# Experts' rows by a scatter in DRAM and VectorE transposes in place of gathers and TensorE transposes, one core of Trainium2

## The chip, the core and the metric

One core of a Trainium2 chip runs the kernel. The metric is the device time in microseconds of one execution. Before the change the median of three runs is 691.87 us (689.24 to 692.97).

## What is computed

Four sequences of 512 tokens with 512 channels go through one layer: a linear attention whose state is trained step by step (a recurrence over 32 mini batches of 16 tokens), a layer norm, then a mixture of eight experts of which each token takes two, beside a shared expert, and a second layer norm.

```python
k, v = heads(x @ Wk.T), heads(x @ Wv.T)           # 16 heads of 32, k rotated
def step(W, (kc, vc)):                             # 32 steps of 16 tokens
    z = kc @ W
    return W - kc.T @ ((z - vc) * inv_n), z
x = layernorm(x + (layernorm(zs) * gamma + beta) @ Wo.T)
probs = softmax(x @ w_gate); w, ids = top_k(probs, 2); w /= sum(w)
expert_e(x) = (silu(x @ gate_e) * (x @ up_e)) @ down_e          # 512 -> 2*256 -> 512
routed = sum over the two experts of w * expert(x)
shared = (silu(x @ g) * (x @ u)) @ down_sh                      # 512 -> 2*1024 -> 512
out = layernorm(x + routed + shared)
```

## The kernel before

All products of the large matrices are made in a fast 32-bit form from a high and a low part: each operand is split by ScalarE (a copy that rounds, "high") and VectorE or GpSimd (the difference, "low"), and TensorE multiplies high by high, high by low and low by high. 24 products of 128x128 by 128x512 are thus one half of a gate block, twelve one bank.

The 2048 tokens are 16 tiles of 128 rows, `x1[:, i, :]`. One function, `stages()`, writes the order of all steps by hand, and each engine's function walks through the same list and issues its own part of every step; so a step's place in the list is its place in the queue of every engine that has a part in it, SP's and GpSimd's too. Signals (`mark`, `on`) tie them together.

1. Recurrence, steps n = 0 to 71. At step n a tile i has its parts at n - 4i = 3 (rows, z), 4 (turn), 5 (statistics, which go through DRAM and back on SP), 7 (output product), 8 (`mix`), 9 (`x1`), 10 (`x1 turn`, TensorE turns the tile for the router), 11 (`logits`). `LAST = 4 * NT - 4 + 11` is the last step. From n = 47 on a budget per step (`SCAN`, `DRAIN`) lets the generator `shared()` lay products of the shared expert between; in the last steps it is 2.3 a step and 2.0 more at one. A half gate or a down product costs 1.3 of it.
2. Routing, `route(e, rt)`, pieces 0 to 18, laid between the products of the shared expert, nearly all on VectorE. Pieces 0 to 7 pick two experts for each token and count them (TensorE sums the counts in piece 7), 8 to 11 give each expert tiles, 12 gives each token its two slots (`SI`, line 867) and weights (`WW`). Pieces 13 to 16 build one-hot matrices from the slots, TensorE multiplies them in two groups of 16 (line 1213, pieces 17 and 18), and the product is the inverse list, `idxu`: which token sits in which slot.
3. Experts. There are 22 tiles of slots, eight wide (four strips of 128 rows) and 14 narrow (one strip); the first seven narrow ones stand between the wide ones in `ORDER`, 15 jobs with 39 strips, and a narrow tile that is not used is skipped by a branch (its products are left out, its strip is still fetched, turned and split). The other seven are rare and have a branch of their own, not entered here. With these inputs five of the narrow jobs have tokens (jobs 1, 3, 5, 7, 9); 11 and 13 have none. For each strip s, step `gather` makes GpSimd fetch 128 rows of `x1d` through `idxu` into one of four places of `xg` (line 1805); step `rows turn` has TensorE turn them into a PSUM bank by four transposes (line 1255), ScalarE copy the high part from there into `RH` or `XH1` (line 1712) and VectorE take the low part (line 1491). A wide job's strips go to the buffer of parity p, and their first copy waits for the gates of the wide job before, which read the same buffer (`row_left`).
   In a job TensorE does the gates (`rows gate`, line 1268: four banks in 2 x 24 products; `strip gate`, line 1281: 12), and then the down products of the job before (`rows down`, line 1305: six for a strip). ScalarE copies each down product out of bank 6 or 7 (line 1726) and SP writes it to `yd` (line 1042). VectorE multiplies gate and up parts (lines 1450, 1496) and takes low parts (1452, 1500); ScalarE and VectorE split the gate weights (1654, 1440), ScalarE and GpSimd the down weights (1659, 1792). During a wide job the one strip of the next narrow job is turned, during a narrow job the four of the next wide job.
4. The last shared products for tiles 8 to 15; GpSimd gathers each token's two rows of `yd` through `SI` (line 1830), VectorE adds them (1508), and the last layer norm ends it.

SP's issues stand in its queue in the order of the list: it waits for a step's signal and only then looks at the next.

## Time and profile before

| | before |
|---|---|
| median of three runs | 691.87 us |
| the profiled execution | 693.32 us |
| its span (first to last instruction) | 691.5 us |
| TensorE busy | 666.4 us |
| VectorE busy | 428.3 us |
| ScalarE busy | 298.9 us |
| GpSimd busy | 295.3 us |
| mean granted clock of TensorE | 0.989 |
| moved by DMA | 92.47 MB |

The profile is of one execution; it took 1.8 us more than its span and stands 1.45 us above the median of the runs. Busy times are of instructions; a matmul's end is modelled, so it is the distance between the starts of two groups that tells how long a group takes. The chain of waits is followed back from the last instruction.

### The profile page before, as it was taken

What the parts mean: (1) busy time and instruction counts of PE and PEld (TensorE: products, weight loads), DVE (VectorE), ACT (ScalarE), POOL (GpSimd) and SP (SyncE); (2) the same over time, 40 slices, a digit from 0 to 9 for tenths busy, and PEclk for the clock granted to TensorE, in tenths of its full rate; (3) what the DMA queues carried; (4) which work ended last, traced back from release to release, by engine and by line L of the source; (5) the groups of instructions that cost most, each with busy time, mean ns of one, the idle gap of its engine ahead of it and who ended that gap; (6) DMA issues with size and microseconds to landing.
All of it is one profiled execution on the core that took longest, in us unless ns stands there. A gap on an engine that the chain in (4) does not pass through costs nothing.

```text
span 691.5 us, 16510 instructions
## 1 busy us (share of the span) xinstructions
PE 666.4 (96%) x6880; PEld 534.6 (77%) x6880; DVE 428.3 (62%) x750; ACT 298.9 (43%) x520; POOL 295.3 (43%) x308
## 2 busy tenths in 40 slices
PE   9889999998999999999999999999999999999994
PEld 7656777776777777787887888888887888888883
DVE  5787766776845345488866544554456267676655
ACT  5534434542654432441123456655677442142232
POOL 0745666766736531011005335343552244726232
PEclk9989999999999999999999999999999999999998
DMA  8210152232351532100063578667657765414212
GB/s 283 83 65 20 50 174 80 85 109 63 112 171 50 171 98 91 45 1 0 1 244 114 177 265 299 199 245 256 207 161 259 261 185 175 123 61 127 72 76 91
DMA packets 65710, 92.47 MB, mean 134 GB/s; under 512 B 16672, under 2 KB 31776, under 8 KB 65632
## 3 DMA queue, kind: packets, MB, share of 16 engines
q1 hardware_dynamic: 59952, 72.76, 31.2%
q0 software_dynamic: 5680, 18.62, 9.5%
q8 instruction: 56, 0.92, 0.5%
q14 instruction: 22, 0.18, 0.1%
HBM read 67.56 MB, written 23.79 MB: 132 GB/s over the span
## 4 chain that ended last, share of the span: by engine, by line
PE 54%; DVE 18%; POOL 9%; issue 7%; ACT 5%; DMA 4%; SPq 0%; DVEq 0%; POOLq 0%; ACTq 0%
PE bank L1305 7%; PE zbank L1268 6%; PE wbank L1268 6%; PE zbank L1181 5%; PE bank L1073 4%; PE bank L1128 4%; PE wbank L1181 4%; PE bank L1194 3%; DVE x L1460 3%; POOL xg L1830 2%; DMA xg<-yd,SI 2%; PE zbank L1281 2%; DVE x L1508 2%; PE bank L1181 2%; PE zbank L1091 2%
## 5 line engine op out<-in xcount | busy, mean ns | idle before, releaser
L1792 POOL TENSOR_TENSOR xl<-RAW,xh 128x1024 fp32r<-128x1024 f32 x23 | 55.5, 2412 | 122.7 <-ACT xh L1659 122.6
L1675 ACT ACTIVATE ah<-sg 128x512 fp32r<-128x512 f32 x48 | 30.3, 632 | 158.4 <-DVE sg L1450 158.4
L1805 POOL DMA_INDIRECT xg<-x1d,idxu x39 | 42.0, 1078 | 69.8 <-DVE idxu L892 41.3
L1440 DVE TENSOR_TENSOR GL<-RAW,GH 128x1024 fp32r<-128x1024 f32 x42 | 50.3, 1223 | 11.0 <-ACT GH L1654 9.6
L1452 DVE TENSOR_TENSOR al<-sg,ah 128x512 fp32r<-128x512 f32 x48 | 34.1, 711 | 33.5 <-ACT ah L1675 33.5
L1194 PE MATMUL bank<-xh,ah 128*128 128x512 f32 x128 | 51.2, 400 | 1.7 <-DVE x L1460 1.0
L1830 POOL DMA_INDIRECT xg<-yd,SI x32 | 35.4, 1106 | 38.6 <-DVE x L1508 24.1
L1073 PE MATMUL bank<-xh,GH 128*128 128x512 f32 x112 | 49.0, 438 | 2.4 <-DVE shuf L1346 2.4
L1194 PE MATMUL bank<-xh,al 128*128 128x512 f32 x128 | 49.9, 390 | 0.0
L1194 PE MATMUL bank<-xl,ah 128*128 128x512 f32 x128 | 49.9, 390 | 0.0
L1450 DVE TENSOR_TENSOR sg<-sg,zbank 128x512 f32<-128x512 f32 x22 | 15.1, 685 | 53.1 <-PE zbank L1268 36.4
L1073 PE MATMUL bank<-xl,GH 128*128 128x512 f32 x112 | 45.6, 407 | 0.1
L1654 ACT ACTIVATE GH<-RAW 128x1024 fp32r<-128x1024 f32 x44 | 45.2, 1056 | 0.0
L1073 PE MATMUL bank<-xh,GL 128*128 128x512 f32 x112 | 45.1, 403 | 0.0
L1460 DVE TENSOR_TENSOR x<-bank,x 128x512 f32<-128x512 f32 x64 | 40.9, 680 | 5.9 <-PE bank L1194 5.8
L1181 PE MATMUL zbank<-XH,GH 128*128 128x512 f32 x112 | 44.1, 394 | 0.2 <-DVE XL L1445 0.2
L1181 PE MATMUL wbank<-XH,GH 128*128 128x512 f32 x112 | 43.8, 391 | 0.0
L1181 PE MATMUL zbank<-XH,GL 128*128 128x512 f32 x112 | 43.6, 389 | 0.0
L1181 PE MATMUL wbank<-XH,GL 128*128 128x512 f32 x112 | 43.6, 389 | 0.0
L1181 PE MATMUL wbank<-XL,GH 128*128 128x512 f32 x112 | 43.6, 389 | 0.0
L1181 PE MATMUL zbank<-XL,GH 128*128 128x512 f32 x112 | 43.6, 389 | 0.0
L1588 ACT ACTIVATE W<-wbank 128x512 f32<-128x512 f32 x31 | 18.5, 597 | 41.7 <-PE wbank L1107 41.7
(302 smaller groups left out, 1773.3 us busy)
## 6 DMA issues: line engine op xcount, KB each, us to landing
RAW<-in_wgu SPq DMA_DIRECT2D x13, 1024.0 KB, 6.5
yd<-RAW SPq DMA_DIRECT2D x39, 256.0 KB, 4.7
RAW<-in_wsgu SPq DMA_DIRECT2D x14, 512.0 KB, 5.1
RAW<-in_wd SPq DMA_DIRECT2D x13, 512.0 KB, 5.8
x<-in_xtok SPq DMA_DIRECT2D x16, 256.0 KB, 3.4
x1d<-x SPq DMA_DIRECT2D x16, 256.0 KB, 2.3
RAW<-in_wsd SPq DMA_DIRECT2D x8, 512.0 KB, 4.8
out_x<-x SPq DMA_DIRECT2D x16, 256.0 KB, 2.0
```

What stands on the lines that cost most here:

```text
L1073: t = e.matmul(bank[b][:], (WL if wl else WH)[:, j, k, hg * 128:hg * 128 + 128], (xl if xlo else xh)[:, k, :], start=(k == 0 and not wl an ...
L1181: t = e.matmul(bank[b][:], (GL if wl else GH)[:, w % 2, k, c:c + 128], (XL if xlo else XH)[q % 2][:, k, :], start=(k == 0 and not wl and n ...
L1194: t = e.matmul(bank[b][:], (al if al_ else ah)[:, ap, k, j * 128:j * 128 + 128], (DL if wl else DH)[:, w % 2, k, :], start=(k == 0 and not ...
L1268: t = e.matmul(bank[b][:], (GL if wl else GH)[:, w % 2, k, c:c + 128], (rowl if xlo else rowh)[p][:, k, :], start=(k == 0 and not wl and n ...
L1305: t = e.matmul(bank[b][:], (al if al_ else ah)[:, p, k, h * 128:h * 128 + 128], (DL if wl else DH)[:, w % 2, k, :], start=(k == 0 and not ...
L1440: e.tensor_tensor(GL[:, w % 2, k:k + 2, :], gate_raw(w, k), GH[:, w % 2, k:k + 2, :].bitcast(F32), ALU.subtract).then_inc(*mark("low", "g" ...
L1452: e.tensor_tensor(al[:, ap, fc, :], sg[:, g, :], ah[:, ap, fc, :].bitcast(F32), ALU.subtract).then_inc(*mark("low", "a", w, q, fc))
L1460: e.tensor_tensor(x1[:, i, :], bank[b][:], x1[:, i, :], ALU.add).then_inc(*mark("acc", w, q, j))
L1654: e.activation(GH[:, w % 2, k:k + 2, :], gate_raw(w, k), ACT.Copy).then_inc(*mark("high", "g", w, k))
L1792: e.tensor_tensor(DL[:, w % 2, :, :], draw[:, raw_of(w), :, :], DH[:, w % 2, :, :].bitcast(F32), ALU.subtract).then_inc(*mark("low p", "d" ...
L1805: e.indirect_dma_start(place(s), None, x1d, bass.IndirectOffsetOnAxis(ap=idxu[:, LINES[s]:LINES[s] + 1], axis=0)).then_inc(*mark(f"dma xg{ ...
L1830: e.indirect_dma_start(xg[:, p, j, :], None, yd, bass.IndirectOffsetOnAxis(ap=SI[:, j, i:i + 1], axis=0)).then_inc(*mark(f"dma ya{p}", i, j))
```

## The change

Instead of the inverse list, the rows themselves are put in the experts' order: as soon as the slots are known (piece 12), GpSimd writes the rows of all 16 tiles through `SI` into an array `xsd` in DRAM, once for each of the two experts: 32 indirect DMAs, tiles 8 to 15 from `x1`, tiles 0 to 7 (whose `x1` has shared products added by then) from a copy reloaded into the two row buffers, first slots before second ones. Slots that no token takes hold rows that SP writes during the recurrence: each finished tile is also written to up to three of the 46 lines of `xsd`. A strip is then a plain read of 128 rows: SP loads it by four DMAs, the quarter g of the channels to the 32 partitions from 32g, so that transposes of 32x32 blocks on VectorE are enough to bring the channels onto the partitions, in an order to which the rows of the gate weights are permuted on the host. VectorE turns the strip into one of two buffers `xt`, ScalarE and VectorE split it from there. The 39 groups of four transposes, pieces 13 to 18 of the routing with their 32 products, and the gathers of `x1d` are gone.

The first four strips are loaded after the scatter and after the loads of weights of jobs 0 and 1; a strip s + 4 is loaded when strip s is turned. In the list a strip's split comes behind the turn of the next one.

The last tile of the recurrence has `mix` and `x1` in the same step as its output product and its turn and logits in the two steps behind, so there are two steps fewer (`LAST` 69 instead of 71), with their budget of fill work.

```diff
-LAST = 4 * NT - 4 + 11
+LAST = 4 * NT - 4 + 9
-        tiles = {d: (n - d) // 4 for d in range(3, 12) if (n - d) % 4 == 0 and 0 <= (n - d) // 4 < NT}
+        tiles = {d: (n - d) // 4 for d in range(3, 12) if (n - d) % 4 == 0 and 0 <= (n - d) // 4 < NT - (d > 7)}
+        if n >= 4 * NT + 4:
+            tiles.update({10: NT - 1} if n == LAST - 1 else {11: NT - 1})
...
             do("wo", tiles[7], left[7])
+            if tiles[7] == NT - 1:
+                do("mix", NT - 1)
+                left[7] = ("mix", NT - 1)
+                do("x1", NT - 1)
...
-        for q_, at in ((0, 49), (1, 69)):
+        for q_, at in ((0, 49), (1, 66)):
...
-        budget += 0 if n < 47 else SCAN[n % 4] if n < 64 else DRAIN + 2.0 * (n == LAST - 2)
+        budget += 0 if n < 47 else SCAN[n % 4] if n < 64 else DRAIN + 1.4 * (n == LAST - 2)
...
-    route, pause = list(range(19)), 0
-    pauses = {6: 1, 16: 6}
+    route, pause = list(range(13)), 0
+    pauses = {6: 1}
...
-            if r == 18:
-                left[4] = ("routed", "index")
-                for s in range(4):
-                    do("gather", s, None)
+            if r == 12:
+                do("scatter")
...
+    for s in range(4):
+        do("rows in", s)
+    def turn_rows(j):
         p = j % 2
         for h, line in enumerate(strips(ORDER[j])):
-            b, s = banks[h], AT_LINE[j] + h
-            do("rows turn", s, p, h, b, left[b], row_left[p])
-            left[b] = ("low", "r", s)
-            place_left[s % 4] = ("turned", "r", s)
+            s = AT_LINE[j] + h
+            do("rows turn", s)
+            if h:
+                do("rows split", s - 1, p, h - 1, row_left[p])
             if s + 4 < len(LINES):
-                do("gather", s + 4, place_left[s % 4])
+                do("rows in", s + 4)
             yield
+        do("rows split", s, p, h, row_left[p])
...
SP:
                 elif step == "x1":
                     i, = a
                     e.wait_ge(*on("x1", i))
+                    for line in range(3 * i, min(3 * i + 3, COLS)):
+                        e.dma_start(xsd[128 * line:128 * line + 128, :], x1[:, i, :]).then_inc(*mark(f"dma x1d{i // 4}", "x", line))
...
                     e.dma_start(ups[:], upd).then_inc(*mark("dma table"))
+                    for h in range(2):
+                        e.wait_ge(*on(f"dma x1d{h}", 4 * h + 3))
+                        e.dma_start(early[h], x1d[512 * h:512 * h + 512, :].rearrange("(t p) n -> p t n", p=128)).then_inc(*mark(f"dma early{h}", h))
...
+                elif step == "rows in":
+                    s, = a
+                    if s == 0:
+                        for j in range(2):
+                            e.wait_ge(*on(f"dma xs{j}", 7))
+                    if s >= 4:
+                        e.wait_ge(*on("rows", s - 4))
+                    for g in range(4):
+                        e.dma_start(place(s)[32 * g:32 * g + 32, :].rearrange("p (m c) -> p m c", m=4),
+                                    xsd[128 * LINES[s]:128 * LINES[s] + 128, 128 * g:128 * g + 128].rearrange("(m i) c -> i m c", m=4)).then_inc(*mark(f"dma xq{s % 4}", s, g))
...
TensorE:
-                elif step == "rows turn":
-                    s, p, h, b, free, after = a
-                    e.wait_ge(*on(f"dma xg{s % 4}", s))
-                    e.wait_ge(*on(*free))
-                    for g in range(4):
-                        t = e.transpose(bank[b][:, g * 128:g * 128 + 128], place(s)[:, g * 128:g * 128 + 128], ident[:])
-                    t.then_inc(*mark("turned", "r", s))
...
VectorE:
                 elif step == "rows turn":
+                    s, = a
+                    e.wait_ge(*on(f"dma xq{s % 4}", s, 3))
+                    if s > 1:
+                        e.wait_ge(*on("low", "r", s - 2))
+                    e.transpose(xt[:, s % 2, :].rearrange("p (c m i) -> p m c i", c=4, m=4), place(s).rearrange("p (m c i) -> p m c i", m=4, c=4)).then_inc(*mark("rows", s))
+                elif step == "rows split":
+                    s, p, h, after = a
                     e.wait_ge(*on("high", "r", s))
-                    e.tensor_tensor(rowl[p][:, :, h * 128:h * 128 + 128], bank[b][:].rearrange("p (a b) -> p a b", a=4),
+                    e.tensor_tensor(rowl[p][:, :, h * 128:h * 128 + 128], xt[:, s % 2, :].rearrange("p (a b) -> p a b", a=4),
                                     rowh[p][:, :, h * 128:h * 128 + 128].bitcast(F32), ALU.subtract).then_inc(*mark("low", "r", s))
...
ScalarE:
+                elif step == "rows split":
+                    s, p, h, after = a
+                    e.wait_ge(*on("rows", s))
                     if h == 0 and after:
                         e.wait_ge(*on(*after))
-                    e.activation(rowh[p][:, :, h * 128:h * 128 + 128], bank[b][:].rearrange("p (a b) -> p a b", a=4), ACT.Copy).then_inc(*mark("high", "r", s))
+                    e.activation(rowh[p][:, :, h * 128:h * 128 + 128], xt[:, s % 2, :].rearrange("p (a b) -> p a b", a=4), ACT.Copy).then_inc(*mark("high", "r", s))
...
GpSimd:
-                elif step == "gather":
...
+                elif step == "scatter":
+                    for q in range(4):
+                        e.wait_ge(*on(f"dma x1d{q}", 4 * q + 3))
+                    for j in range(2):
+                        e.wait_ge(*on("routed", "slots", j))
+                        for i in (*range(8, NT), *range(8)):
+                            if j == 0 and i in (0, 4):
+                                e.wait_ge(*on(f"dma early{i // 4}", i // 4))
+                            rows = early[i // 4][:, i % 4, :] if i < 8 else x1[:, i, :]
+                            e.indirect_dma_start(xsd, bass.IndirectOffsetOnAxis(ap=SI[:, j, i:i + 1], axis=0), rows, None).then_inc(*mark(f"dma xs{j}", i))
```

## Rows read from the trace of the kernel before

**Rows 1.** The page: busy us, share of the span, instructions, of TensorE.
```profile
PE 666.4 (96%) x6880; PEld 534.6 (77%) x6880; DVE 428.3 (62%) x750; ACT 298.9 (43%) x520; POOL 295.3 (43%) x308
```

**Rows 2.** TensorE's waits, 260 to 400 us: total us, times, longest.
```profile
PE zbank L1268 <- DVE RL L1491: 0.6, 1, 0.6
```

**Rows 3.** The chain of waits: start us, us, what.
```profile
357.21 1.70 PE bank L1213 x16
...
379.60 5.69 PE zbank L1268 x24
...
391.23 0.44 PE bank L1255 x4
...
401.47 5.48 PE zbank L1268 x24
...
458.92 1.36 PE bank L1305 x6
...
460.72 2.77 PE zbank L1281 x12
...
470.53 5.48 PE zbank L1268 x24
...
504.96 1.36 PE bank L1305 x6
...
513.97 5.48 PE zbank L1268 x24
```

**Rows 4.** VectorE in order of time: start us, us, instruction, idle before.
```profile
292.95 0.28 DVE L734 TENSOR_REDUCE red<-logits 128x16 f32<-128x128 f32 x1
...
320.13 0.17 DVE L798 TENSOR_TENSOR ce<-ce 128x12 f32<-128x12 f32 x1
...
320.41 2.38 DVE L798 TENSOR_TENSOR ce<-ce 128x8 f32<-128x8 f32 x1
...
333.37 0.17 DVE L867 CAST SI<-red 128x16 uint32<-128x16 f32 x1
```

**Rows 5.** GpSimd in order of time, the same columns.
```profile
320.36 2.40 POOL L1792 TENSOR_TENSOR xl<-RAW,xh 128x1024 fp32r<-128x1024 f32 x1 [14.90 <-ACT xh L1659]
...
365.53 0.95 POOL L1805 DMA_INDIRECT xg<-x1d,idxu  x1 [0.30 <-issue]
```

**Rows 6.** The page: a costly group (mean ns), and DMA issues (us to landing).
```profile
L1805 POOL DMA_INDIRECT xg<-x1d,idxu x39 | 42.0, 1078 | 69.8 <-DVE idxu L892 41.3
...
x1td<-x1f SPq DMA_DIRECT2D x12, 256.0 KB, 2.5
...
xg<-yd,SI POOLq DMA_INDIRECT x32, 3.7
```

**Rows 7.** SP's lines 1042 and 955: ns of an issue, least/median/most.
```profile
L1042 SPq DMA_DIRECT2D yd<-RAW x39: 319/332/467, 397.8 to 555.9; - x39
...
L955 SPq DMA_DIRECT2D x1td<-x1f x12: 370/432/460, 70.5 to 287.1; - x12
```

**Rows 8.** VectorE's line 1390: ns of one, least/median/most.
```profile
L1390 DVE STREAM_TRANSPOSE zT<-zst x16: 696/701/702, 46.8 to 260.2; 128x512 f32<-128x512 f32 x16
```

**Rows 9.** VectorE and ScalarE in order of time, around 465 us.
```profile
463.95 0.42 DVE L1496 TENSOR_TENSOR sg<-sg,zbank 128x256 f32<-128x256 f32 x1 [0.87 <-ACT sg L1716]
464.60 0.69 DVE L1491 TENSOR_TENSOR RL<-bank,RH 128x512 fp32r<-128x512 f32 x1 [0.23 <-ACT RH L1712]
...
464.94 0.60 ACT L1712 ACTIVATE RH<-wbank 128x512 fp32r<-128x512 f32 x1
466.24 0.60 ACT L1726 ACTIVATE RAW<-bank 128x512 f32<-128x512 f32 x1 [0.69 <-PE bank L1305]
...
468.16 1.06 ACT L1654 ACTIVATE GH<-RAW 128x1024 fp32r<-128x1024 f32 x1
```

**Rows 10.** Busy times by stretch: us, then each engine; PEclk, DMA share, GB/s.
```profile
30.00:35.00 5.00, 3.78 (x70) 2.64 (x70) 3.65 (x7) 3.87 (x9) 2.52 (x2) 0.66 0.00 0
...
446.00:469.00 23.00, 23.00 (x113) 19.12 (x112) 11.58 (x16) 13.94 (x23) 10.19 (x8) 1.00 0.74 249
```

More of the change, by code:

```diff
@@ L362, in routing @@
             r = route.pop(0)
-            do("route", r, {7: (left[6], left[7]), 17: left[4]}.get(r))
+            do("route", r, (left[6], left[7]) if r == 7 else None)
             if r == 7:
                 left[6], left[7] = ("routed", "before"), ("routed", "totals")
-            if r == 18:
-                left[4] = ("routed", "index")
-                for s in range(4):
-                    do("gather", s, None)
+            if r == 12:
+                do("scatter")
             pause = pauses.get(r, 0)
@@ L448, in stages @@
             do("load gate", 6)
-        if n == 2:
-            next(first_turns)
+    next(first_turns, None)
     split_down(4)
@@ L647, in program @@
         sg = sb(ctx, "sg", [2, 512])
-        oneh = [R[:].rearrange("p k n -> p (k n)").rearrange("p (t n) -> p t n", t=NT) for R in (RH, RL)]
+        early = RH[:].bitcast(F32), RL[:].bitcast(F32)
         incl = c0
-        iota = cst[:, 16 + 2 * RT + NT:16 + 2 * RT + NT + 128]
         plan = stages()
@@ L1206, in tensor @@
                         e.matmul(bank[7][:, 0:128], ups[:, 128:256], chosen, start=True, stop=True).then_inc(*mark("counts", "totals"))
-                    if rt in (17, 18):
-                        if rt == 17:
-                            e.wait_ge(*on("routed", "rows"))
-                            e.wait_ge(*on(*free))
-                        j = rt - 17
-                        for i in range(NT):
-                            t = e.matmul(bank[4][:, 0:IDX], oneh[j][:, i, :], onec[:, j, i, :], start=(rt == 17 and i == 0), stop=(rt == 18 and i == NT - 1))
-                        if rt == 18:
-                            t.then_inc(*mark("counts", "index"))
                 elif step == "tiles used":
@@ L1227, in tensor @@
                                 e.wait_ge(*on("dma rare y", n - 1))
-                            e.wait_ge(*on("dma rare x", n))
+                            e.wait_ge(*on("rare dve", "rows", n))
                             for g in range(4):
-                                t = e.transpose(bank[4][:, g * 128:g * 128 + 128], RAW[:, 1, g * 128:g * 128 + 128], ident[:])
+                                t = e.transpose(bank[4][:, g * 128:g * 128 + 128], xt[:, 0, g * 128:g * 128 + 128], ident[:])
                             t.then_inc(*mark("rare pe", "x", n))
@@ L1706, in scalar @@
                         e.wait_ge(*on("dma rare y", RARE[-1]))
-                elif step == "rows turn":
-                    s, p, h, b, free, after = a
-                    e.wait_ge(*on("turned", "r", s))
+                elif step == "rows split":
+                    s, p, h, after = a
+                    e.wait_ge(*on("rows", s))
                     if h == 0 and after:
                         e.wait_ge(*on(*after))
-                    e.activation(rowh[p][:, :, h * 128:h * 128 + 128], bank[b][:].rearrange("p (a b) -> p a b", a=4), ACT.Copy).then_inc(*mark("high", "r", s))
+                    e.activation(rowh[p][:, :, h * 128:h * 128 + 128], xt[:, s % 2, :].rearrange("p (a b) -> p a b", a=4), ACT.Copy).then_inc(*mark("high", "r", s))
                 elif step == "strip act":
@@ L1825, in gpsimd @@
                             e.wait_ge(*on(f"dma y{s % 4}", s))
-                        e.wait_ge(*on("turned", "r", len(LINES) - 1))
+                        e.wait_ge(*on("rows", len(LINES) - 1))
                     if i > 1:
@@ L1881, in constants @@
                                      np.tile([512.0 * (n % 4) + 128.0 * (n // 4) for n in range(8)], (128, 1)),
-                                     np.tile([n if n < FULL else FULL + (n - FULL) // 4 for n in range(RT)], (128, 1)), np.tile(np.arange(RT), (128, 1)),
-                                     np.arange(NT)[None, :] * 128 + rows[:, None], np.tile(np.arange(128), (128, 1))], 1).astype(np.float32),
+                                     np.tile([n if n < FULL else FULL + (n - FULL) // 4 for n in range(RT)], (128, 1)), np.tile(np.arange(RT), (128, 1))], 1).astype(np.float32),
             "up": np.concatenate([(rows[:, None] < rows[None, :]), np.ones((128, 128))], 1).astype(np.float32)}
@@ L1894 @@
     left = np.concatenate([np.arange(256), np.arange(256, 512).reshape(2, 2, 64)[:, ::-1].reshape(-1)])
+    turned = np.arange(512).reshape(4, 4, 32).transpose(1, 0, 2).reshape(-1)
     xo = np.ascontiguousarray(x.reshape(4, 32, 16, 512).transpose(1, 0, 2, 3).reshape(2048, 512))
```

64 lines of the change are left out of this document (14 added, 50 removed).

## The prediction

> **What bounds the kernel now.** I read the busy times first: TensorE is busy 666.4 of 691.5 us [rows 1], so a change pays only if it takes work out of TensorE's order or shortens one of its waits. The waits of TensorE come next: from the middle of the kernel on only small ones are left, and the one at the change is 0.6 us, for the first strips' split on VectorE [rows 2]. The chain of waits then gives the order [rows 3]: after the recurrence TensorE runs without a pause through the shared experts, two blocks of 16 index products and the last down products, and at 379.60 it starts the gates of the first job (a job is an expert's tile: four strips wide, or one narrow). From there it alternates wide job, narrow job. TensorE sets the time, but between two jobs the other engines are close behind: the narrow jobs 11 and 13 have no tokens and give TensorE almost nothing, and at the first of them the next wide gates begin at 513.97, 9.0 us after the wide gates before ended (504.96).
>
> **What is removed on TensorE.** The index products: two groups of 16 at 1.70 us [rows 3], 3.4 us. The transposes of the strips: 39 groups of four at 0.44 us [rows 3], 17.2 us, all on TensorE's path. The first four (1.76 us) stand before the first gates, with the wait of 0.6 us. So TensorE could reach the first wide gates at 379.60 - 3.4 - 1.76 - 0.6 = 373.8, and if nothing else became late the kernel would gain 21.2 us. The index arithmetic on VectorE (steps 13 to 16 and 18) lies beside shared experts and is worth nothing by itself.
>
> **When the slots are known.** The routing arithmetic begins at 292.95 and has the first slots at 333.37 [rows 4]. The end of the recurrence is drawn together: steps 64 up to the last pay 8 x 2.3 + 2.0 = 20.4 us of fill work in the planner's units before, 6 x 2.3 + 1.4 = 15.2 after, a unit being about a microsecond of TensorE. TensorE's work stays, only its order changes; the routing may start up to 5.2 us earlier in it. But two splits of gate weights now stand ahead of its first operation on VectorE, so I take 3.5 us: slots at about 330. The last tile's own chain (mix, normalise, turn, logits) gets less cover; from the order, some four half gates (1.36 us each, as the six-product piece in [rows 3]) lie between its output product and its turn, against some 4.3 us of mix, statistics and scaling, so I cost that at nothing, at worst 1 us.
>
> **The scatter.** 32 indirect DMAs stand in a row on GpSimd, each of 128 rows. The trace has no scatter; the nearest row is the gather of the same size and engine: 0.95 us plus 0.30 us of issue at best [rows 5], 1.08 us plus 0.30 in the mean [rows 6]. Bounds: 32 x 1.25 = 40.0 us, and 1.6 us each (51 us) if writing through the list is slower; below the gather's best I see no reason. I take 1.36: 43.5 us, since VectorE's work holds some of them up. 330.2 + 43.5 = 373.7 for the last issue, and 3.7 us from issue to landing [rows 6] bring 376.4. Nothing needed soon stands behind it on GpSimd but the down weights' split of job 0 (2.4 us, [rows 5]), which the wait below hides.
>
> **The first strips.** SP waits for the last scatter and only then issues the first strips: 4 x 4 DMAs. One issue of SP takes 0.33 us for a y strip and 0.43 us for the turned x1 [rows 7]; 0.46 with the gap: 7.4 us for sixteen. The last lands 2.2 us later (2.5 for the x1td write [rows 6]), then VectorE turns it (0.70 us, the row of the z transpose [rows 8]), ScalarE copies it (0.60) and VectorE splits it (0.69) [rows 9]: 376.4 + 7.4 + 2.0 + 2.0 = 387.8. TensorE is ready at 373.8: a stall of 14 us takes the place of 0.6. Bounds: 8 us (slots at 329, 40 us, 0.38 us per issue), 22 us (51 us of scatter). After smaller pauses early in the kernel the granted clock was 0.66 over 5 us [rows 10], which is part of the time at the 1.2 GHz level; one such stretch after the stall costs 0.34 x 5 = 1.7 us. I add 1.5 (0 to 3).
>
> **The strips in the steady part.** Let G be the end of a wide job's gates, 458.92 in the pair I read, where the narrow down product starts. Now: TensorE does the narrow job's down product (1.36), the strip gate (2.77), four groups of transposes, four down products (24 products, 5.50) and a small turn of 0.22; the next wide gates start at 470.53, G + 11.6 [rows 3]. Without the transposes TensorE would be there at G + 9.85. But the four strips of the next wide job must be turned and split in just this stretch, because their buffer is free only at G, and VectorE's order puts turns two to four behind the strip's product with the activation (463.95 now, 0.42 us [rows 9]; 0.44 earlier after: ends at G + 5.0). Behind it, with two buffers for turned strips and each turn waiting for the split of two strips before: turn 5.7, split 6.4, turn 7.1, split 7.8, turn 8.5, ScalarE's copy 9.1. ScalarE's order matters most. Its copy of the y strip 1 frees a bank for down product 3, and stands behind that copy and behind a weights' copy of 1.06 us [rows 9]: 10.1, then the y copy (0.60, overlapping by 0.1) to 10.6, down product 3 to 12.0, turn, gates at G + 12.2. Instead of 1.76 us earlier they start 0.6 later. So do they in the four full pairs and, by the same count, after the first wide job (now 10.2 us from 391.2 to 401.47). In the jobs 11 and 13, where TensorE has least, I get G + 10.9 against 9.0: 1.9 each. Sum of seven: 5 x 0.6 + 2 x 1.9 = 6.8. Against it, one transposition inside each of seven wide gates goes, 7 x 0.44 = 3.1: net +3.7.
>
> There is a further price. The split read a PSUM bank and one SBUF tile; now it reads two SBUF tiles. At 320.36 GpSimd subtracts two tiles for 2.40 us, and VectorE's 8-element addition of 320.41, two SBUF inputs, takes 2.38 us where its neighbours take 0.17 [rows 4, 5]. GpSimd's split of the down weights stands about 3.5 to 6 us behind G, so the first of the four splits can be held 0.8 us, seven times: up to 5.6. The bounds are 0 and 5.6; I take 3.3, as the two do not always meet. The Trainium skill ("SBUF — State Buffer", section "SBUF: two separate sides") states such a lock: the pair of ports is held for a whole instruction by whichever came first of a GpSimd operation and a VectorE operation with two SBUF inputs. By that rule the extra would be the whole 5.6, without it 0; the trace agrees with it at 320.4. The steady part is then +7.0 (from -4, if my chain is 1.5 us too long seven times, to +9.3).
>
> **Edits at nothing.** The 46 writes that fill the scattered array during the recurrence: 3 more issues of 0.43 us per tile on SP. They stand behind the statistics' round trip of the next tile and before the write of the turned tile and the next row's load, which have a half step or more; cover gone, 1.3 us for a tile. The reload of eight early tiles is needed by the ninth scatter, 45 us later. In the steady part SP issues 20 more DMAs for a pair of jobs, 9 us of about 22: it has the room, and strips are loaded four ahead. GpSimd loses its gathers, which nobody waited for. The permuted weights cost nothing on the chip.
>
> **Sum.** -3.4 - 1.76 - 0.6 + 14.0 + 1.5 + 7.0 = +16.7. The profiled execution took 693.32 us, 1.45 above the median of the runs, 691.87; on the median this is 708.5. About 0.5% (3.5 us) can be told from no change.
>
> **The rivals and their chances.**
> (1) My forecast, 701 to 716 us: 0.60.
> (2) Faster: the steady part keeps TensorE's gain. This decides between the wide gates: if VectorE and ScalarE finish four strips by G + 9.85, 7 x 0.44 + 28 x 0.44 = 15.4 us stay, and the sum is -5.8 + 15.5 - 15.4 = -5.7: 686. For it: over a whole pair VectorE is busy half of the time, 11.58 of 23 us [rows 10]. Against: the turns can't start before G, and the y copy stands behind the last strip's copy. 0.13, with the faster mixtures.
> (3) The scatter is covered: slots earlier and TensorE's cover longer than 57 us. It needs 14 us that I don't find; -5.8 + 7 = +1: 693. 0.08. With both (2) and (3), 671: 0.02.
> (4) The scatter is slower than the gather, 1.6 us or more each: 8 us on top, 717 to 725. 0.10.
> (5) Something between (1) and (3), 695 to 700: 0.07.
> The change does what it says in any of them: no transposes of strips on TensorE.
>
> **Numbers.** Faster is (2) with the double case, 0.15; within 0.5% (3), 0.08; slower 0.77. The range 690 to 720 leaves out the most of (2) and the end of (4).
>
> **What would show it.** The waits of TensorE must have a first one of 8 to 22 us before the first wide gates, for VectorE's split, and the granted clock must dip behind it. GpSimd must show 32 scatters over 40 to 51 us from about 330. TensorE's chain must show the wide gates about 12.2 us or more behind the end of the ones before in full pairs, with waits for ScalarE's y copy or VectorE's splits. I am wrong if the first wide gates start before 381, if they follow at G + 10, or if scatters take other than 1.25 to 1.6 us.

## The result

The changed kernel takes 722.15 us (median of four runs, 720.67 to 724.68) against 692.36 for the kernel before: ratio 1.0457, interval 1.0425 to 1.049. That is slower by some 30 us where 16.7 were forecast, and 2 us above the upper end of the range. The profiled execution took 721.94 us with a span of 720.1. Unaltered, the same kernel took still more when it was run again twice beside later experiments (738.7 and 739.2 us, e9 and e13): there is a second effect, which the profile of this section does not have and many of the experiments below do.

The page of the changed kernel, busy us of each engine (answers to [rows 1]), two costly groups, and two of its groups of DMA issues ([rows 6]; KB each, us to landing):

```profile
PE 659.8 (92%) x6692; PEld 521.2 (72%) x6692; DVE 450.1 (62%) x779; ACT 302.7 (42%) x520; POOL 285.0 (40%) x301
...
L1783 POOL TENSOR_TENSOR xl<-RAW,xh 128x1024 fp32r<-128x1024 f32 x23 | 55.4, 2408 | 220.6 <-ACT xh L1650 220.5
...
L1288 PE MATMUL bank<-xh,ah 128*128 128x512 f32 x74 | 31.9, 431 | 18.0 <-ACT RAW L1717 15.4
...
xsd<-x SPq DMA_DIRECT2D x46, 256.0 KB, 2.4
xg<-xsd SPq DMA_DIRECT2D x156, 64.0 KB, 2.1
```

TensorE is busy 6.6 us less, but it now idles 60 us instead of 25. Its waits say where (the whole kernel; total us, times, longest; [rows 2]):

```profile
PE bank L1288 <- ACT RAW L1717: 15.4, 14, 1.8
PE zbank L1251 <- issue: 7.9, 1, 7.9
PE bank L1158 <- ACT logits L1618: 3.2, 1, 3.2
PE bank L1193 <- DVE GL L1423: 2.9, 1, 2.9
```

Before, the longest kind came to 2.5 us, and of these four only the wait for y copies was there, once, with 0.4 us. Now there are 15.4 us for ScalarE's y copies, twice in each of seven pairs of jobs; 7.9 us before the first wide gates; 3.2 us in the recurrence's tail; 2.9 us within the last shared products. The chain gives the stages ([rows 3]):

```profile
375.47 7.31 PE bank L1193 x24
382.78 7.93 issue
390.71 8.46 PE zbank L1251 x24
...
417.53 5.49 PE zbank L1251 x24
...
441.80 5.50 PE zbank L1251 x24
...
452.75 1.36 PE bank L1288 x6
...
457.39 0.39 ACT sg L1707
...
458.14 0.71 DVE xt L1478
458.85 1.02 DVE RL L1482
...
462.64 0.95 ACT GH L1645
463.59 0.58 ACT RAW L1717
464.17 0.04 issue
464.22 1.66 PE bank L1288 x6
...
531.00 1.67 DVE RL L1482
...
563.13 5.50 PE zbank L1251 x24
```

The kernel before reaches the gates of job 14, the last, here:

```profile
534.35 5.47 PE zbank L1268 x24
```

| stage, us | before | after | difference |
|---|---|---|---|
| start to the first slots | 333.37 | 333.74 | +0.4 |
| slots to the first wide gates | 46.23 | 56.97 | +10.7 |
| first wide gates to those of job 14 | 154.75 | 172.42 | +17.7 |
| those to the end | 157.2 | 157.0 | -0.2 |

So the span grew by 28.6 us (691.5 to 720.1). Slots, scatter and first turn, in order of time on VectorE, GpSimd and VectorE again ([rows 4, 5]):

```profile
333.74 0.17 DVE L869 CAST SI<-red 128x16 uint32<-128x16 f32 x1
```
```profile
334.81 1.24 POOL L1796 DMA_INDIRECT xsd<-x,SI  x1 [7.62 <-DVE pr L865]
...
374.81 1.03 POOL L1796 DMA_INDIRECT xsd<-RL,SI  x1 [0.30 <-issue]
```
```profile
382.60 0.71 DVE L1478 STREAM_TRANSPOSE xt<-xg 128x512 f32<-128x512 f32 x1 [4.00 <-DMA xg<-xsd]
383.23 1.18 DVE L1423 TENSOR_TENSOR GL<-RAW,GH 128x1024 fp32r<-128x1024 f32 x1
384.33 0.68 DVE L1443 TENSOR_TENSOR x<-bank,x 128x512 f32<-128x512 f32 x1
```

A scatter costs what a gather does: 0.96 + 0.30 us, 32 of them in 41.0 us, one above my lower bound of 40.0; the first starts 1.1 us behind the slots. The clock is the last view (columns as in [rows 10]). TensorE idled through 385:390, and in 390:395, the five us in which the gates begin, the granted clock is 0.50, all of it at the 1.2 GHz level.

```profile
360.00:380.00 20.00, 17.06 (x69) 13.66 (x68) 9.06 (x13) 5.44 (x8) 12.18 (x13) 0.91 0.86 343
...
385.00:390.00 5.00, 0.00 (x0) 0.00 (x0) 4.88 (x10) 2.01 (x4) 0.00 (x0) 0.63 0.44 128
390.00:395.00 5.00, 4.29 (x10) 3.45 (x11) 0.61 (x1) 0.83 (x1) 2.36 (x1) 0.50 0.98 286
```

### The profile page after: what moved, and what is told of

It is laid out like the page before. It is cut to its first block, busy times and chain, and to the rows that moved or that the text cites. A ratio compares the mean times of both kernels' runs of the same rounds, so it can differ in the third digit from the quotient of the medians.

```text
span 720.1 us, 16357 instructions
## 1 busy us (share of the span) xinstructions
PE 659.8 (92%) x6692; PEld 521.2 (72%) x6692; DVE 450.1 (62%) x779; ACT 302.7 (42%) x520; POOL 285.0 (40%) x301
## 4 chain that ended last, share of the span: by engine, by line
PE 51%; DVE 20%; issue 8%; POOL 8%; ACT 7%; DMA 4%; SPq 0%; DVEq 0%; POOLq 0%; ACTq 0%
PE zbank L1251 7%; PE zbank L1180 6%; PE bank L1193 5%; PE wbank L1180 5%; PE bank L1072 5%; PE bank L1127 5%; PE wbank L1251 5%; PE bank L1288 3%; DVE x L1443 2%; DVE xt L1478 2%; POOL xg L1819 2%; PE zbank L1264 2%; DMA xg<-yd,SI 2%; PE zbank L1090 2%; DVE x L1499 2%
## 5 line engine op out<-in xcount | busy, mean ns | idle before, releaser
L1193 PE MATMUL bank<-xh,ah 128*128 128x512 f32 x128 | 51.5, 402 | 4.9 <-DVE GL L1423 2.9
L1288 PE MATMUL bank<-xh,ah 128*128 128x512 f32 x74 | 31.9, 431 | 18.0 <-ACT RAW L1717 15.4
L1366 DVE TENSOR_TENSOR r<-zbank,mask 128x256 f32<-128x256 f32 x32 | 13.4, 420 | 36.1 <-PE zbank L1090 36.1
```

What stands on the lines that cost most here:

```text
L1193: t = e.matmul(bank[b][:], (al if al_ else ah)[:, ap, k, j * 128:j * 128 + 128], (DL if wl else DH)[:, w % 2, k, :], start=(k == 0 and not ...
L1288: t = e.matmul(bank[b][:], (al if al_ else ah)[:, p, k, h * 128:h * 128 + 128], (DL if wl else DH)[:, w % 2, k, :], start=(k == 0 and not ...
```

## The experiments

All edits start from the changed kernel. "Gates" is the start of the first wide gates, "jobs" the stretch from there to the gates of job 14; in the changed kernel 390.7 and 172.4. These are read from one profiled execution each. The experiments were run in five sets, after that of the result, each with the kernel before beside it: e1, e2, e3 and e5; e4 and e6 to e8; e9 to e12; e13 to e16; e17 and e18. The slots come at 333.74 in the changed kernel's first profile and at 336.28 and 336.60 in those of e9 and e13, so a difference of 2 or 3 us in when the gates begin says nothing by itself.

**e1, the tail as it was.**

```diff
-LAST = 4 * NT - 4 + 9
+LAST = 4 * NT - 4 + 11
```
(and the last tile's steps and the budget as before)

> The changed kernel with the recurrence's last tile as before (two half steps between, 20.4 of fill). My theory: the drawn-together tail costs TensorE 3.2 us of waiting for the logits' copy behind the last x1 and about 2 us at the lower clock, and brings the slots no earlier (333.7). Undone, the shared products before the experts end about 5 us earlier, at 367.5 instead of 372.5, but the slots come at 333 to 334 too, so the first wide gates, bound by the scatter and the loads, stay at 390 to 391 and the time stays within 1.5 us of the changed kernel's 722. Rival: the tail's loss is on the path to the end; then 5 us less, 717. Second rival: the shorter tail does bring the slots earlier; then undoing it makes it slower by up to 5 us, 727.

723.04 us, ratio to the kernel before 1.0464 (1.0429 to 1.05). The last shared products start at 370.18 instead of 375.47, so the new tail does cost TensorE 5 us; but they stand ahead of a wait of 11.3 us for the strips, and the slots come no later (332.6). From the slots to the gates it takes 56.2 us against 57.0, and the time is the same within the noise: the 5 us of the tail do not reach the end. (The jobs take 176.5 us here, because the granted clock fell at two more wide gates, whose first half takes 6.8 and 6.7 us instead of 5.5.)

**e2, TensorE turns the strips again, scatter kept.**

```diff
-e.transpose(xt[:, s % 2, :]..., place(s)...)          # VectorE
+for g in range(4): e.transpose(bank[b][:, g * 128:g * 128 + 128], place(s)[:, g * 128:g * 128 + 128], ident[:])   # TensorE
```
(and each strip loaded by one DMA of whole rows; ScalarE and VectorE split it from the bank, as before the change)

> The changed kernel (scatter and new tail kept), but each strip is loaded by one DMA of whole rows and turned by TensorE into a PSUM bank as before. My theory: VectorE's turns are what makes the jobs slow. The stretch from the first wide gates to the last ones' start goes from 172.4 back to about 155 us, less 0 to 3 us by the clock; the first gates start about 3 us earlier (4 issues instead of 16, 5.5 us less, 2 us more for the turns); together 722 - 17 - 3 = 702. Rival: the jobs are slow because of the added DMA traffic or SP's queue; then the stretch stays above 165 us and the time above 712.

705.58 us, ratio 1.0228 (1.0202 to 1.0254): the chain has

```profile
390.58 5.71 PE zbank L1254 x24
...
545.35 5.47 PE zbank L1254 x24
```

Jobs take 154.8 us, the kernel before's 154.75. The whole +17.7 of that stage comes with VectorE's turns. What the edit takes away with them is the split's second SBUF input (e4 has its price) and the quarter loads (e5: they cost the jobs nothing), and the clock: the first half of the first gates takes 5.71 us instead of 8.46. The first gates are as late as before the edit.

**e3, four banks for the wide down products.**

```diff
-b, y = 6 + h % 2, (AT_LINE[j] + h) % 4
+b, y = (6, 7, 4, 5)[h], (AT_LINE[j] + h) % 4
```

> The changed kernel, but the down products of a wide job go round the banks 6, 7, 4, 5 instead of 6, 7, 6, 7 (4 and 5 are free without TensorE's turns). My theory: between two jobs TensorE waits for ScalarE's y copy to free a bank (14 waits, 15.4 us). Without that wait the next wide gates wait for the last strip's split and the low part of the weights, ready some 12.2 us behind the end of the gates before instead of 13.34. So 1.0 to 1.2 us per wide job, seven times: 714 to 715. Rival: y copies are the bound by themselves; then a pair falls from 24.29 to 23 or less and the time to 708 or less. Second rival: another wait ends at the same moment; then the waits move from the down products to the gates and the time stays at 722.

717.79 us, ratio 1.0396 (1.0361 to 1.043). Expected were 714 to 715 us. The waits for the y copies are gone, and most of their time stands elsewhere:

```profile
PE zbank L1251 <- DVE GL L1423: 14.0, 7, 2.9
```

The wait was a symptom: what the gates wait for is the end of VectorE's list. A full pair takes 23.5 us instead of 24.29, so 0.8 us are gained and not 1.0 to 1.2. Two of the pairs take 25.07 instead: TensorE idles up to 2.9 us before the gates, and at two of them the granted clock is then 0.79 (438:446 and 534:542) and the first half of the gates takes 7.3 us. Without these two times 1.6 us the time would be 714.6, by my estimate from these rows: part of what the order gains, the clock takes back.

**e5, one plain load for a strip instead of four quarters** (the strips' channels are then out of order; all durations stay).

```diff
-for g in range(4): e.dma_start(place(s)[32 * g:32 * g + 32, :]..., xsd[..., 128 * g:128 * g + 128]...)
+e.dma_start(place(s), xsd[128 * LINES[s]:128 * LINES[s] + 128, :])
```

> The changed kernel, but each strip is loaded by one DMA of 2 KB rows instead of four of 512 B pieces, and turned by VectorE all the same; the channels are then not in the order of the weights, so the gates multiply other numbers. My theory: in the steady part nothing changes (pairs of 24.3 us), since strips arrive long before they are turned; before the first gates SP issues 4 instead of 16 DMAs, 5.6 us less, so they start at about 386 (VectorE's seven operations behind the first strip take 8 us from its landing) instead of 390.7. Time 717 to 719. Rival: the quarters slow the jobs too (packets, SP's queue); then pairs fall below 23.5 us and the time below 712. Second rival: the load's issue is not on the path; then 722.

721.56 us, ratio 1.0471 (1.0433 to 1.0508). A miss of mine. From the slots to the first gates it takes 56.3 us against 57.0: SP's sixteen issues were not what the first gates waited for. (The profile is of an execution of 717.86 us, whose slots came at 330.35.) VectorE needs 8.1 us from its first turn to the gates in either kernel, because weight splits and sums of the shared block stand between its turns, as the three rows from 382.60 on show.

**e4, GpSimd's subtraction for the down weights of jobs 2 to 14 cut to 8 elements.**

```diff
-e.tensor_tensor(DL[:, w % 2, :, :], ...)
+e.tensor_tensor(DL[:, w % 2, 0:1, 0:8], ...)      # GpSimd
```

> From the changed kernel; GpSimd's subtraction for the low parts of the down weights of jobs 2 to 14 is cut to 8 elements (their low parts stay stale), all else as it is. Theory (the engines' common port costs part of it): the first split after a wide job's gates is 0.4 us shorter in each of the pairs in use and 1.1 us in the two that are not, 3 to 5 us in all: 717 to 719 us. Rival (the lock costs nothing that the end sees): 721 to 723 us.

732.28 us, ratio 1.0589 (1.0548 to 1.063): slower, against both expectations. Its profile has two parts. The jobs behave as expected:

```profile
504.98 5.47 PE zbank L1251 x24
...
528.82 5.49 PE zbank L1251 x24
...
575.10 5.47 PE zbank L1251 x24
```

A full pair takes 23.84 us instead of 24.29, the two with an idle narrow job 23.1 each instead of 24.2: the lock costs 3.9 us in these six. All jobs take 167.9 us instead of 172.4, but the other 0.6 is the clock: it lies in the first transition, where the splits take 0.65 us in both kernels, and the first half of the gates 7.85 us instead of 8.46. In the changed kernel the first split behind G takes 1.02 us in a full pair and 1.67 in an idle one, where later ones take 0.58 or 0.59 (as pieces of the chain). In e4 none takes over 0.70. The Trainium skill ("SBUF — State Buffer", section "SBUF: two separate sides") says that the pair of ports is held for the whole of an instruction; the trace agrees, and 3.9 of the 5.6 us that my count gave as a limit are there, 1.1 at each idle job.

But the first gates come at 407.2 instead of 390.7. All engines except GpSimd all but stand still in the second half of the scatter; I call this the stop:

```profile
355.00:360.00 5.00, 4.17 (x17) 2.83 (x16) 0.00 (x0) 0.60 (x1) 3.78 (x5) 1.00 0.50 204
...
360.00:380.00 20.00, 5.09 (x9) 2.38 (x9) 1.38 (x2) 0.63 (x1) 13.97 (x15) 0.54 0.54 209
```

(These two rows are of e13 below, the changed kernel itself; e4's has 4.70 us of TensorE in 360:380.) The stop begins with the DMA engines half free.

**e6, the same work in another order**: two strips of the next wide job turned one job ahead, four banks, the narrow strip's products first, down weights split last.

```diff
+turn_row(AT_LINE[j + 2] + h)                # h = 0, 1, beside the wide job's own gates
-strip_gate(j) behind the first turn, split_down(j + 5) in every job
+strip_gate(j) first, split_down(j + 4) and (j + 5) behind strip_turn(j)
```

> From the changed kernel, same work in another order: the first two strips of a wide job are turned one job earlier, while VectorE idles beside the gates before; four banks for the down products; the splits of the down weights go behind the narrow job's turn; the products of the narrow strip come first on TensorE; at the start all products of the last shared block and the weight splits stand ahead of the turns. Theory (the turns' 0.6 us each count only because they stand in VectorE's list between a wide job's gates and the next): the next gates start about 10 us after the last instead of 13.3, a full pair takes 20.5 to 21.5 us instead of 24.3, the first gates come at 387 to 388 instead of 390.7, and the time is 690 to 697 us. Rival (VectorE has too much to do in a pair whatever the order): pairs stay above 23.5 us and the time above 714 us.

**e7, e6 with a shared block moved ahead of the experts.**

```diff
 for _ in down(3, 1): pass
+for _ in gate(3, 2): pass
+for _ in down(3, 2): pass                   # its sums wait for the scatter
```

> e6 with one more move: the gates and down products of shared block 3 for the third token quarter, 16 us of products that the kernel runs at its end, stand ahead of the experts, where TensorE waits for scatter and strips. Theory (the wait for the scatter is a hole on TensorE's path that any ready work fills): the first wide gates start at 390 to 393 us, the last part is 16 us shorter, and the time is 10 to 14 us under e6's, 678 to 686 us. Rival (the products moved there only push the strips' turn back, or the x1 sums that must wait for the scatter hold VectorE): gates not before 398 us and at most 5 us under e6.

**e8, e2 with that block moved.**

> The changed kernel with TensorE's turns in place of VectorE's (e2, 705.6 us) and the same block of 16 us ahead of the experts. Theory: the hole is the rest of e2's loss; its time falls by 12 to 16 us to 690 to 694 us, even with the kernel before. Rival (the hole is not TensorE's to fill): 700 us or more.

729.71 us (1.0563, 1.0509 to 1.0616), 742.54 (1.0743, 1.0683 to 1.0803) and 729.9 (1.057, 1.0526 to 1.0614). All three stopped as e4 did. Their jobs can still be read: e6's take 163.6 us (405.90 to 569.48), so the order and the four banks together are worth 8.8 of the 17.7. The four banks alone gave 3.2 in e3, where the jobs take 169.2, and 1.3 are the clock of the first gates (7.12 us instead of 8.46); the pairs are at 23.5 instead of the 20.5 to 21.5 expected. e8's take 154.8.

**e9, the changed kernel unaltered, and e10, e6 unaltered.**

> The changed kernel itself, unaltered, as a control. In e4, e6, e7 and e8 every engine stood still from about 352 us, with only half of the DMA engines' time taken, and TensorE was busy for 5 us of 360:380; the stop comes ahead of the first instruction that those edits touch. Theory A (instructions are fetched late while the scatter runs, and how late is a matter of the chip or of chance, not of the edit): the unaltered kernel shows the same stop on this chip, or its runs scatter between 721 and 733 us. Theory B (the edits' code brings it about): 720 to 724 us with 16 to 17 us of TensorE in 360:380, as before.

> e6 unaltered, beside the changed kernel on the same chip. Theory A: where the changed kernel is not stopped here, this one is not either, and it takes 690 to 700 us; where both are stopped, it stays 3 us or so under it. Theory B: stopped again (TensorE under 8 us in 360:380) whatever the changed kernel does.

738.72 us (1.0655, 1.06 to 1.071) and 731.58 (1.0576, 1.0539 to 1.0613). So the stop is not brought about by an edit; that much of theory A holds. The kernel before is not touched by it: beside the three sets with the stop it took 690.66, 692.12 and 691.78 us. Against its own control e6 gains 7.1 us.

**e11 and e12, e7 and e8 with the branch over the rare tiles behind the shared products.**

```diff
-do("tiles used"); do("rare tiles", ahalf[3, 0])      # behind down(3, 0)
+do("tiles used"); do("rare tiles", ahalf[3, 2])      # behind down(3, 2)
```

> e7 with the branch over the rare tiles (and the first weight loads behind it) moved behind all shared products that stand ahead of the experts, so that TensorE, VectorE and ScalarE come to it after the scatter. Theory A1 (the late fetch belongs to the jump): the stop at 352 to 380 us is gone, TensorE works through to about 390 us, the first wide gates start at 393 to 398 us and the time is 680 to 692 us. Theory A2 (any fetch of instructions is late during the scatter): TensorE stops as before and the time is 735 us or more.

> e8 (turns on TensorE, a shared block ahead of the experts) with the branch moved as in e11. Theory A1: 688 to 698 us. Theory A2: 725 us or more, as e8 (729.9).

742.19 us (1.0724, 1.0687 to 1.076) and 731.43 (1.055, 1.0497 to 1.0604): nothing gained. The jump over the rare tiles is not it.

**e13, the control again, with e14 to e16: bytes, outstanding transfers, or the kind of issue.**

```diff
-e.indirect_dma_start(xsd, IndirectOffsetOnAxis(SI...), rows, None)
+e.indirect_dma_start(xshort, IndirectOffsetOnAxis(SI...), rows[:, 0:64], None)   # e14
+if n >= 4: e.wait_ge(*on(f"dma xs{n % 4}", n - 4))                               # e15, ahead of the issue
+e.dma_start(xsd[128 * line:128 * line + 128, :], rows)                           # e16
```

> The changed kernel unaltered, the control for e14 to e16. If the stop belongs to the chip: either 720 to 725 us with 16 us or more of TensorE in 360:380, or 730 to 742 us with under 8 us of it there; the other three are read against this one.

> The scatter writes only the first 64 of each row's 512 channels, to a tensor of its own (an eighth of the bytes; 32 issues as before); the experts then run on rows that are not scattered. Theory (the bytes in flight hold the other engines' instructions off): no stop on any chip, TensorE over 16 us in 360:380, and 718 to 724 us where the control stops at 730 or more. Rival (the indirect issues on GpSimd do it, whatever they carry): it stops as the control does, within 5 us of it.

> Each indirect transfer of the scatter waits until the fourth before it has landed, so that at most four are outstanding. Theory (a queue that grows behind the issues holds the instructions off): the stop is gone or under 5 us, the scatter ends up to 5 us later, and the time is 722 to 730 us on any chip. Rival (four are enough to hold them off, or the queue never was longer): as the control, or above it.

> GpSimd issues the same 32 transfers of 256 KB as plain writes of a line of xsd each, rows in order; the experts run on rows that are not sorted. Theory (scattered rows are what the memory or the queue is slow with): no stop, and the plain issues take GpSimd's time otherwise; 710 to 722 us. Rival (bytes are bytes): where the control stops, this stops too, within 5 us of it.

e13: 739.19 us (1.0687, 1.0633 to 1.074), on the chip that had run e1, e2, e3 and e5 without a stop; so it is not a matter of the chip either. e14: 738.7 (1.0702, 1.0642 to 1.0762), e15: 740.13 (1.0695, 1.0629 to 1.0761), e16: 714.57 (1.0353, 1.0297 to 1.0409). In e14 the DMA engines are almost idle and TensorE crawls all the same, one product in 2.8 us:

```profile
360.00:380.00 20.00, 5.89 (x11) 2.88 (x12) 1.92 (x3) 0.63 (x1) 11.15 (x12) 0.50 0.12 40
```
```profile
363.27 0.59 PE L1181 MATMUL zbank<-XH,GH 128*128 128x512 f32 x1 [1.51 <-issue]
366.07 0.59 PE L1181 MATMUL zbank<-XL,GH 128*128 128x512 f32 x1 [2.21 <-issue]
```

In e16 the same bytes go out by plain issues, eight in 4.57 us, and nothing stops; its gates start at 382.17:

```profile
360.00:380.00 20.00, 16.01 (x70) 12.62 (x68) 15.33 (x24) 8.23 (x13) 0.00 (x0) 1.00 0.76 221
```

So the bytes do not matter (e14). e15 says less than it was meant to: its scatter takes as long as the control's (the last issue 39.5 us behind the first, 39.6 in e13), so four transfers were about all that was ever outstanding, and nothing was limited. What e16 leaves out are the indirect issues, but also their length. In all eleven stopped profiles TensorE first waits 20 to 23 us behind the first indirect issue, and goes on at its pace 5 to 6 us behind the start of the last one. e16's 32 issues are over after 17.4 us, before that point. That plain issues of the same length would not stop the others is not shown; that the stop goes with a long row of indirect issues is.

Are instructions held off? The DMA queues of 345:375 seem to say so, e16 first, then e13, then e9 (packets, MB, share):

```profile
q0 software_dynamic: 1270, 4.12, 38.8%
q8 instruction: 2, 0.03, 0.5%
q14 instruction: 2, 0.02, 0.1%
```
```profile
q0 software_dynamic: 1881, 6.13, 50.1%
```
```profile
q0 software_dynamic: 1688, 5.52, 45.5%
q1 hardware_dynamic: 835, 1.68, 22.2%
q14 instruction: 2, 0.02, 0.2%
```

The queues that bring instructions delivered nothing in these 30 us of e13, and the same holds for e14 and e15. But in the eight stopped kernels from e4 to e12 the two packets of q14, which land at 353 and 356 in the changed kernel's first profile, land between 362 and 372, in the middle of the stop, and it goes on. In e9 they land at 367 and 368, and TensorE behind them:

```profile
374.11 0.59 PE L1180 MATMUL zbank<-XH,GL 128*128 128x512 f32 x1 [2.21 <-issue]
376.92 0.59 PE L1180 MATMUL zbank<-XH,GH 128*128 128x512 f32 x1 [2.22 <-issue]
```

The packets also come behind the work and not ahead of it: VectorE's product at 350.87 in the first profile (line 1433) comes at 362.99 in e9 and 376.68 in e13, each time 2 to 4 us before the first packet of q14, and SP's next weight load moves with it (350.80, 362.91, 376.60). So late packets can as well be a result of late engines. The Trainium skill ("Advanced Engine Details and Errata", section "ISA Cache") gives an engine 32 KB for instructions, TensorE 128 KB, in lines of 256 instructions, and only two lines. That an engine without its next line must stop is my inference; no run here shows the cache, and e9 shows TensorE crawling on for 12 us after the packets.

**e17 and e18, three pauses in the scatter; e18 on top of e8.**

```diff
+if j: e.wait_ge(*on("dma xs0", 7))                  # after 16 issues
+if i == 0: e.wait_ge(*on(f"dma xs{j}", 15))         # after 8 and 24
```

> The changed kernel with three pauses in the scatter: after 8, 16 and 24 issues GpSimd waits until all before have landed (some 4 to 5 us each). Theory (GpSimd's issues hold the others' instructions off only while they run back to back): packets of the queue of instructions land in the pauses, TensorE is busy for over 12 us of 360:380 instead of 5, the scatter ends 12 to 15 us later, at about 390, and the time is 728 to 736 us where an unpaused one stops (739). Rival (what is held off stays off until the last issue): TensorE under 8 us in 360:380 and 748 to 756 us.

> e8 (TensorE turns the strips, the shared block of 16 us stands ahead of the experts) with the same three pauses. Theory: TensorE works through the scatter, the first wide gates start at 397 to 403 us instead of 425.8, the jobs keep e8's pace, and the time is 698 to 706 us against e8's 729.9. Rival: 735 us or more.

732.15 us (1.0616, 1.0575 to 1.0656) and 705.89 (1.0253, 1.0206 to 1.03), both within the times of the theory. e17's scatter ends at 386.9, and neither kernel stops; TensorE of e17 and of e18:

```profile
360.00:380.00 20.00, 17.26 (x75) 13.64 (x74) 9.04 (x13) 5.33 (x8) 10.62 (x11) 1.00 0.65 256
```
```profile
360.00:380.00 20.00, 19.20 (x85) 15.63 (x84) 9.22 (x14) 3.82 (x7) 12.07 (x12) 1.00 0.62 246
```

With the same work, e18's gates start at 400.51 instead of e8's 425.79, and its time is 24 us lower. That the pauses did this is not shown. Their sign in the theory did not come: the two packets of q14 land at 354.5 and 355.5 in e17, behind the first pause (2.0 us, to 345.9) and before the second (6.5 us, from 356.6), while issues run back to back. And the stopped kernels slow down 20 to 23 us behind the first issue, here 354 to 357, so at that point only the first pause can have helped. e17 and e18, run together, may have been spared by chance, as the changed kernel's first runs and e1, e2, e3 and e5 were. Against that: in the three sets before, on three chips, every kernel stopped but e16. A control beside e17 and e18 would have settled it; there was none.

## Why the prediction failed, point by point

**What bounds the kernel**: right. TensorE sets the time, and between jobs the others are close behind.

**TensorE's work removed**: right in kind. 188 matrix instructions went, 20.6 us by the forecast's prices; busy time fell by 6.6, since some of the rest ran at the lower clock (mean 0.972 instead of 0.989). None of it reached the end, since TensorE waits at both places.

**Slots at 330**: 333.74 in the profile of the result, and 333.9 in the mean of the 18 profiles with the new tail (330.4 to 337.9), against 333.37 and 332.6 in the two with the old one: no earlier. The tail's shorter budget did not become earlier routing. The cost of the last tile's own chain, taken as nothing and at worst 1 us, failed too: the logit rows' turn waits 3.2 us for a copy that stands on ScalarE behind the last tile's scaling, and the clock falls to 0.93 and 0.90 (260:300), 5 us of TensorE together. As e1 shows, it cost the end nothing.

**The scatter, 43.5 us**: 42.1 from the slots to the end of the last issue, 41.0 of them issues, near its lower bound, which made good 1.4 of the 3.5 us lost before.

**The first strips, 11.4 us from the last landing to the gates**: 11.7 from SP's first issue at 379.02, but the reason was wrong (e5): VectorE's list, not SP's issues. Together first gates at 390.7 against 387.8 forecast.

**The clock, 1.5 us**: the first half of the first gates takes 8.46 us, where at the full clock it takes 5.47: 3.0 us, at the bound.

**The steady part, +7.0**: this is the step that failed. It took 14.7: of the 17.7 us of its stage 3.0 are the clock. The whole sum, from the table of stages:

| term, us | forecast | measured |
|---|---|---|
| to the first wide gates | +8.2 | +11.1 |
| clock at the first gates | +1.5 | +3.0 |
| steady part | +7.0 | +14.7 |
| the end | 0 | -0.2 |
| sum | +16.7 | +28.6 |

So 7.7 of the 11.9 us that are missing are the steady part's. By its own rows:

| | forecast, with a seventh of the lock | measured |
|---|---|---|
| four full pairs, each | +0.6 | +1.3 |
| two pairs with an idle narrow job, each | +1.9 | +3.8 |
| the first transition | +0.6 | +2.0, and 3.0 of the clock |

In a full pair the gates start at G + 13.3, not G + 12.2: the second strip's turn begins 0.4 us later, the lock adds 0.4, and the last down product takes 1.66 us and not 1.36, since it is waited for to its end. The lock, 3.3 of the forecast, is 3.9 (e4). The chain itself, 3.7, is 10.8: the mechanism was right, VectorE's turns behind G (e2 takes all of it back), and it was sized too small, most of all where the narrow job is idle. There I had G + 10.9, because TensorE has least to do, and it is G + 13.3 (525.59 to 538.89), the same as in a full pair: the chain that the gates wait for runs over VectorE and ScalarE, and the lock is longer there (1.67 us for the first split).

**The rivals**: the scatter slower than the gather did not happen; that the time, 722.15, landed in its span of 717 to 725 is chance. The steady part did not keep the gain; only e6 goes a way towards it, half way back to the old pace, with its order and its four banks.

**Not foreseen at all**: the stop. It costs 17 us where it comes (e9 and e13 against 722.15), nearly as much as the whole loss of the jobs, and no row of the kernel before shows it: its gathers stand in groups of at most four at that place. What brings it about stays open.

## What to carry to other kernels

Moving work from a busy engine to a half idle one gains nothing where the idle one's list puts it in the one stretch that everybody waits for; read the free time in that stretch, not over the period. Be wary of a long row of indirect transfers back to back while other engines have work: here it cost 17 us in three of the five sets of runs that had it. Whether gaps between them help is not shown (e18 is 24 us under e8, with the doubt told there). Run the unaltered kernel again beside later experiments before reading a difference of a few per cent: without e9 the stop would have been put down to the edits.

## What the hardware showed unexpectedly

During 32 indirect issues on GpSimd, 1.26 us apart, all other engines nearly stood still, in three of the five sets of runs whose scatters had no pauses, the result's among the five; in the first two (the result, and e1, e2, e3, e5) nothing of the kind happened. The stop began 20 to 23 us behind the first issue and ended 5 to 6 us behind the last. TensorE made one product in 1.4 to 3.5 us, and its granted clock fell to 0.50; the DMA engines were 12% busy in e14 and 54 to 90% in the others (360:380). The queues of instructions delivered nothing from 345 to 375 in e13 to e15, but two packets of q14 in the eight others. With an eighth of the bytes it came all the same (e14); with plain issues, which were over in 17.4 us, it did not (e16). With three pauses of 2.0, 6.5 and 3.5 us it was not seen, without a control. What in the issues holds the others off, and why the first two sets were spared, stays open.

No version here beats the kernel before: the nearest are e2 (705.6) and e18 (705.9).
